# A gated recurrence on one core: the input's products cut into four column tiles, and TensorE's loop cut from sixteen steps to four

## The reference

```python
def step(h, x_t):
    fused = sigmoid(concat([x_t, h]) @ w_W + w_b)
    hidden_state, output_state = split(fused, 2)
    memory_state = x_t @ wx_W + wx_b + hidden_state * (h @ wh_W + wh_b)
    h_new = output_state * h + (1.0 - output_state) * tanh(memory_state)
    return (h_new, h_new)
return x + scan(step, cond_1024, x over time)
```

## Time and profile before

| | us |
|---|---|
| median of 3 runs | 1894.34 (1892.4 to 1894.72) |
| the profiled execution, its own time | 1895.98 |
| its span in the trace | 1893.4 |
| busy in the span: PE / PEld / DVE / ACT / POOL | 1859.9 / 1465.7 / 1169.8 / 821.2 / 371.0 |

### The profile page before, as it was taken

The page is one execution under the profiler, slowest core; times in us unless marked ns, Lnnn a source line. Parts: engine busy times, 40 slices in busy tenths (PEclk is TensorE's granted clock), DMA queues, the critical chain, the costliest instruction groups (busy, mean ns, idle before and its releaser), DMA issues.

```text
span 1893.4 us, 124703 instructions
## 1 busy us (share of the span) xinstructions
PE 1859.9 (98%) x52320; PEld 1465.7 (77%) x52320; DVE 1169.8 (62%) x6153; ACT 821.2 (43%) x3983; POOL 371.0 (20%) x1540
## 2 busy tenths in 40 slices
PE   8999999999999999999999999999999999999998
PEld 6777777777777777777777777777777777777776
DVE  3666666666666666666666666666666666666665
ACT  3444444444444444444444444444444444444444
POOL 0111111111111111111111111111111111111111
PEclk9999999999999999999999999999999999999999
DMA  4000000000000000000000000000000000000000
GB/s 152 15 4 15 15 15 15 9 9 15 15 15 15 4 15 15 15 15 4 15 15 15 15 9 9 15 15 15 15 4 15 15 15 15 4 15 15 9 9 9
DMA packets 36083, 29.94 MB, mean 16 GB/s; under 512 B 1616, under 2 KB 34384, under 8 KB 35664
## 3 DMA queue, kind: packets, MB, share of 16 engines
q1 hardware_dynamic: 35664, 23.10, 3.9%
HBM read 14.70 MB, written 8.39 MB: 12 GB/s over the span
## 4 chain that ended last, share of the span: by engine, by line
PE 96%; DVE 2%; DMA 1%; ACT 1%; SPq 0%; issue 0%; POOL 0%; POOLq 0%
PE ps L192 73%; PE ps L181 23%; DVE turned L284 1%; DMA x_sb<-in_x 1%; DVE h L307 0%; ACT h_by L241 0%; DVE pre_z L292 0%; DVE pre_r L288 0%; ACT h L246 0%; SPq L146 0%; SPq L152 0%; SPq L143 0%; SPq L150 0%; SPq L148 0%; SPq L149 0%
## 5 line engine op out<-in xcount | busy, mean ns | idle before, releaser
L192 PE MATMUL ps<-wh,h 128*8 128x128 f32 (+2 forms) x49152 | 1443.2, 273 | 22.5 <-DVE h L307 19.2
L192 PEld LDWEIGHTS ps<-wh,h 128*8 128x8 f32 x49152 | 1073.4, 90 | 260.1 <-DVE h L307 44.0
L284 DVE STREAM_TRANSPOSE turned<-ps 128x128 f32<-128x128 f32 (+1 forms) x2048 | 575.1, 281 | 510.6 <-PE ps L192 483.6
L237 ACT ACTIVATE m_by<-pre_r 128x16 f32<-128x16 f32 x1024 | 223.4, 218 | 894.5 <-DVE pre_r L288 894.5
L181 PEld LDWEIGHTS ps<-x_sb,wx 128*128 128x128 f32 x3168 | 392.3, 192 | 161.8 <-issue 161.8
L181 PE MATMUL ps<-x_sb,wx 128*128 (+1 forms) x3168 | 483.9, 292 | 5.6 <-DMA wx<-in_w_x 5.6
L362 POOL TENSOR_TENSOR add<-turned,bias_h 128x16 f32<-128x16 f32 x1024 | 237.4, 232 | 881.4 <-DVE turned L284 881.4
L307 DVE TENSOR_TENSOR_SCAN h<-h_by,h 128x48 f32<-128x48 f32 x1024 | 263.5, 257 | 152.9 <-ACT h L246 152.6
L241 ACT ACTIVATE h_by<-pre_z 128x16 f32<-128x16 f32 x1024 | 230.2, 225 | 160.0 <-DVE pre_z L292 131.2
L375 POOL TENSOR_TENSOR y<-x_sb,h 128x32 f32<-128x32 f32 x512 | 133.4, 261 | 637.5 <-DVE h L307 637.5
L246 ACT ACTIVATE h<-m_pre 128x32 f32<-128x32 f32 x1024 | 237.6, 232 | 0.0
(11 more groups left out here) (6 smaller groups left out, 0.6 us busy)
## 6 DMA issues: line engine op xcount, KB each, us to landing
x_sb<-in_x SPq DMA_DIRECT2D x32, 256.0 KB, 4.6
out_h<-y SPq DMA_DIRECT2D x32, 256.0 KB, 2.7
wx<-in_w_x SPq DMA_DIRECT2D x6, 512.0 KB, 5.8
wh<-in_w_h SPq DMA_DIRECT2D x4, 768.0 KB, 11.3
bias_x<-in_b_x SPq DMA_DIRECT2D x1, 6.0 KB, 3.2
bias_h<-in_b_h SPq DMA_DIRECT2D x1, 2.0 KB, 3.1
h<-in_h SPq DMA_DIRECT2D x1, 16.0 KB, 3.6
```

The lines of the kernel that those rows point to most:

```text
L192: mm = pe.matmul(ps[Q * j:Q * j + B, bank, 0:cols], h_of(s - 1 if s else S, k), wh[:, k, j, at:at + cols], start=(k == 0), stop=(k == KC - 1),
L237: act.activation(m_by[:, o, :, 1], pre_r[:, o, :], ACT.Sigmoid).then_inc(r_ready[o], 1)
L284: return dve.transpose(turned[:, o, g0:g1].rearrange("p g c q -> p (g c) q"), ps[:, bank, at:at + cols].rearrange("p (c q) -> p c q", q=Q))
```

## The change

What changes, engine by engine:

- **TensorE, x's products.** Each product is cut into four, 32 outputs each, one per column tile. A product `32x128` then has a stationary operand of 128 by 32 and 128 moving columns. Every step has exactly 3 of the old products, so 12 of the new, and the last step of a block has them too. They use three PSUM banks in turn, not two.
- **TensorE, the loop** has a body of four steps. So that its addresses are fixed, each of the four steps r reads x's weights from its own place `wx_step[:, r]` and its own copy of the next block's x, `x_next[:, r]`.
- **SP's queue** loads `wx_step` for every step (three chunks, 192 KB) four steps ahead, once the step that used the place has ended it (`x_used`, or `x_product` for the fourth), and the four copies `x_next` once a block. The x of two blocks ahead is loaded as before.
- **h** is a ring of four places, and VectorE waits every four steps for POOL's `y_added` of the step just before. Until now it waited every eight, for a step eight further back. `y` has two buffers, and POOL waits at each block's start for `x_loaded`, which TensorE did before.

```diff
+    RING = 4
-    X_FROM = [-(-len(x_list) * s // (STEPS - 1)) for s in range(STEPS)] + [len(x_list)]
-    X_PLAN = [x_list[X_FROM[s]:X_FROM[s + 1]] for s in range(STEPS)]
+    X_EACH = len(x_list) // STEPS
+    X_UNITS = RING * X_EACH // KC
...
+        x_next = sb("x_next", [P, RING, KC, TOK])
+        wx_step = sb("wx_step", [P, RING, X_EACH, P])
-        h = sb("h", [P, STEPS, HALVES, HALF])
-        y = sb("y", [P, KC, STEPS, B])
+        h = sb("h", [P, RING, HALVES, HALF])
+        y = sb("y", [P, 2, KC, STEPS, B])
...
+            for r in range(RING):
+                load_wx(r)
+                sp.dma_start(x_next[:, r], x_flat[:, :, TOK:2 * TOK]).then_inc(x_next_loaded[r], 16)
             sp.dma_start(x_sb[:, :, TOK:2 * TOK], x_flat[:, :, TOK:2 * TOK]).then_inc(x_loaded, 16)
...
+            def x_product_of(u, k, w, moving):
+                for j in range(TILES):
+                    at = slice(Q * j, Q * (j + 1))
+                    mm = pe.matmul(ps[at, X_BANK + u % X_UNITS, 0:TOK], w[:, at], moving,
+                                   start=(k == 0), stop=(k == KC - 1), tile_position=(0, Q * j))
+                if k == KC - 1:
+                    mm.then_inc(x_product, 1)
+                return mm
...
+            def x_products(i, s):
+                pe.wait_ge(wx_step_loaded[s], held(pe, i * 16 + 16))
+                pe.wait_ge(x_next_loaded[s], held(pe, (i // (STEPS // RING)) * 16 + 16))
+                for n in range(X_EACH):
+                    u, k = divmod(s * X_EACH + n, KC)
+                    if k == 0:
+                        pe.wait_ge(xg_ready, held(pe, i * X_UNITS + (UNITS - X_UNITS + u + 1)))
+                    last = x_product_of(u, k, wx_step[:, s, n, :], x_next[:, s, k, :])
...
-            with nc.Fori(0, BLOCKS, engines=(mybir.EngineType.PE,), hint_back_edge=True) as i:
...
-                pe.wait_ge(x_loaded, pe.snap(i * 16 + 16))
-                for s in range(STEPS):
+            with nc.Fori(0, T // RING, engines=(mybir.EngineType.PE,), hint_back_edge=True) as i:
+                t0 = pe.snap(i * RING)
+                for s in range(RING):
                     step(t0, s)
-                    x_products(X_PLAN[s], nxt_block, unit0)
+                    x_products(i, s)
...
-                if s % Y_HALF == 0:
-                    dve.wait_ge(y_added, held(dve, t0 + (s + Y_HALF)))
+                if s % RING == 0:
+                    dve.wait_ge(y_added, held(dve, t0 + (s + STEPS)))
```

More of the change, by code:

```diff
@@ L103, in build @@
         x_loaded = sem("x_loaded")
+        x_next_loaded = [sem(f"x_next_loaded{r}") for r in range(RING)]
+        wx_step_loaded = [sem(f"wx_step_loaded{r}") for r in range(RING)]
         y_stored = sem("y_stored")
@@ L117, in build @@
         x_product = sem("x_product")
+        x_used = [sem(f"x_used{r}") for r in range(RING - 1)]
         r_summed = halves("r_summed")
@@ L152, in _, with load_wx @@
                 sp.dma_start(wh[:, k], w_h[:, k]).then_inc(wh_loaded, 16)
-            sp.dma_start(x_sb[:, :, TOK:2 * TOK], x_flat[:, :, TOK:2 * TOK]).then_inc(x_loaded, 16)
-            def store(i):
+            def load_wx(s):
+                sp.dma_start(wx_step[:, s % RING], wx_flat[:, s * X_EACH:(s + 1) * X_EACH])\
+                    .then_inc(wx_step_loaded[s % RING], 16)
+            for r in range(RING):
+                load_wx(r)
+                sp.dma_start(x_next[:, r], x_flat[:, :, TOK:2 * TOK]).then_inc(x_next_loaded[r], 16)
+            sp.dma_start(x_sb[:, :, TOK:2 * TOK], x_flat[:, :, TOK:2 * TOK]).then_inc(x_loaded, 16)
+            with sp.Fori(0, BLOCKS) as i:
+                after = sp.snap((i + 2) % BLOCKS)
+                cols = bass.ds(sp.snap(after * TOK), TOK)
+                sp.wait_ge(x_loaded, sp.snap(i * 16 + 16))
+                sp.dma_start(x_sb[:, :, cols], x_flat[:, :, cols]).then_inc(x_loaded, 16)
+                for s in range(STEPS):
+                    if s % RING == 0:
+                        turn = sp.snap(i * (STEPS // RING) + (s // RING + 1))
+                    if s % RING < RING - 1:
+                        sp.wait_ge(x_used[s % RING], turn)
+                    else:
+                        sp.wait_ge(x_product, sp.snap(i * UNITS + (s // RING + 1) * X_UNITS + UNITS))
+                    load_wx((s + RING) % STEPS)
+                    if s >= STEPS - RING:
+                        sp.dma_start(x_next[:, s % RING], x_flat[:, :, cols]).then_inc(x_next_loaded[s % RING], 16)
                 sp.wait_ge(y_added, sp.snap(i * STEPS + 2 * STEPS))
@@ L167, in _ @@
[L167 to L170, removed]
+                             y[:, bass.ds(sp.snap(i % 2), 1)].rearrange("p a c t b -> p (a c) (t b)"))\
+                    .then_inc(y_stored, 16)
+            sp.wait_ge(x_loaded, (BLOCKS + 1) * 16)
+            for r in range(RING):
+                sp.wait_ge(wx_step_loaded[r], (T // RING + 1) * 16)
+                sp.wait_ge(x_next_loaded[r], (BLOCKS + 1) * 16)
@@ L172, in _ @@
+            sp.wait_ge(y_stored, 16 * (BLOCKS + 2))
         @block.tensor
         def _(pe):
[L174 to L179, removed]
-                        pe.wait_ge(wx_loaded[u * WX_PARTS // UNITS], 16)
[L181 to L184, removed]
+            def x_product_of(u, k, w, moving):
[6 more added lines that the diff above has]
+                return mm
@@ L364, in hidden, with add_x @@
                     .then_inc(hm_ready[o], 1)
-            def add_x(s, t0, nxt, after):
+            def add_x(s, t0, which, after):
                 if s == 0:
@@ L382, in step @@
                     hidden(o, s % 2, nxt)
-                add_x(s, t0, nxt, held(pool, t0 + (s + 2)))
+                add_x(s, t0, which, held(pool, t0 + (s + 2)))
             pool.sem_inc(y_added, STEPS)
```

49 lines of the change are left out of this document (25 added, 24 removed).

## The result

The changed kernel takes 1825.47 us (median of 4 runs, 1824.59 to 1825.9), the kernel before 1893.87 in the same series. The ratio is 0.9639, with a 95% interval of 0.9622 to 0.9656. The forecast was 1827.

The account below looks back on a forecast made before the run. TensorE was taken to bound steps with products of x, the recurrence, only 0.18 us shorter, the step without. From the 1894.3 us median: minus 87 for blocks, plus 19 for jumps, plus 1 for start and end, gives 1827 us (range 1812 to 1845).

Parts of the forecast that it names:

- Bound: TensorE bounds steps with products of x (3.61 us for three); the recurrence bounds the step without, its own period 3.47 us.
- x in column tiles: x slot: six quads take 0.66 us, 32-column loads hide, and up to about 0.3 us of tiling switches a step goes.
- The sum for a block: Block of 16 steps: 58.23 us becomes 55.52, so 2.71 less, and 87 less over 32 blocks.
- The jumps, +19 us: TensorE's four-step loop: the queue gets through the jump late, costing 0.15 us at each of 127 jumps.
- VectorE's wait, costed at nothing: VectorE's first transpose waits for POOL's addition every fourth step; 0.24 us of slack, so no cost.
- Loads and start: Weight loads on SP's queue stay hidden; x for POOL lands at 27 us; start and end add 1 us together.
- The hidden jump: Rival, chance 0.27: at TensorE's loop all goes as forecast but without the 19 us for jumps, giving 1808 us.
- the slot's 0.21 us is no matter of tiling: Rival, chance 0.07: it belongs to each stream's first weights; x slot stays 0.87 us, giving 1917, or 1879 with jumps hidden.
- The fetch of instructions (0.08): Rival, chance 0.08: each TensorE loop jump waits for one or two instruction packets of 1.1 us, giving 1950 to 2090 us.

Follow-up runs that it names:

- the run with five: Changed kernel with two more of x's products in each step, in column tiles, into a bank nobody reads: 1934.74 us, ratio 1.0213.
- the 14-page body: Changed kernel with a 16-step TensorE body, x's weights resident, and six of x's twelve products in four steps: 1825.91 us, ratio 0.9645.

## Why the prediction was right

**Bound.** Right. The step without products of x told what the recurrence allows, 3.47 us; measured are 3.48, with TensorE idle before its h passes. Two products in the slot changed nothing, and from the run with five follows the engine's own period with three, 3.27 us.

**x in column tiles.** Right, and close. The way between the two tilings was priced at up to about 0.3 us a step. The engine's own period with three products is 3.61 on the whole array and 3.27 in tiles, so it is 0.34. The quad of 0.11 us came as the rows of h had it, and the 32-column loads hide: four loads of 110 ns and four matmuls share each 0.11 us. The rule of the Trainium skill (TensorE: Matmul & The Clock Gate, Part 3, The mechanism) that loads overlap only where the row groups differ does not hold here, since all these loads use all 128 rows.

**The sum for a block** was -87 us for a step of 3.47. With 3.477, the mean distance of VectorE's first transposes in the undisturbed steps, it is -83.

**The jumps, +19 us.** This step failed: the h pass behind a jump was to start 0.19 us late, and it starts on time (3.48 us after the one before). The jumps cost 0. Two numbers in it were off, how far the queue runs ahead and what the branch takes. Here are the jump's instructions on TensorE's queue (ns min/median/max, start us), for the earlier trace rows:

```profile
L252 PEldq ALU_OP  x1: 32/32/32, 1005.3 to 1005.3; - x1
L252 PEldq COMPARE_BRANCH  x1: 216/216/216, 1005.4 to 1005.4; - x1
L252 PEldq BRANCH_PREFETCH_HINT  x1: 31/31/31, 1005.7 to 1005.7; - x1
L252 PEldq FUSED_REGOPS  x1: 50/50/50, 1005.8 to 1005.8; - x1
```

The queue comes to the jump at 1005.3, when the last of x's quads is still 0.5 us from its start (1005.27 plus 0.55). I had taken 0.33, from 16 records. 20 would have been right. And it is through at 1005.85, since the branch takes 216 ns. The h pass wants it at 1006.08. 375 ns was the price in a body whose pages are fetched anew, not of a branch as such. The prediction took it for free of any fetch. The kernel before fetched 13 pages in each turn, its branches took 375 ns in the median, those of the 14-page body 448, and those of the two bodies that stay in the store 216.

**VectorE's wait, costed at nothing.** This failed too: 0.07 us in steps 4, 8 and 12, 96 times, 7 us. The price stood in the trace of before. There the wait had its second place in step 8, and this row of VectorE's timeline is that step:

```profile
1046.31 0.32 DVE L284 STREAM_TRANSPOSE turned<-ps 128x128 f32<-128x128 f32 x1 [0.95 <-PE ps L192]
```

It has 0.95 us of idle time where the other steps' transpose has 0.88. It cost nothing then, because the slot of x hid it: the distance of the first transposes is 3.68 us up to that step and 3.54 behind it, around the 3.61 of the others. I had asked whether POOL was in time, and not what the wait itself costs.

**Step 2** of each block loses 0.06 to 0.07 us in VectorE's scan of half 0, 2 us in all. It does so in every run that the recurrence bounds, those with a body of 16 included; only where every step has the second wait does it add nothing. The cause stays open.

**Loads and start.** The loads are hidden with the short body: no wait in the changed kernel's trace ends on `wx_step` or `x_next`. The first x for POOL came at 29 us and not 27, and start and end cost 3 us, not 1: the second step began 1.9 us later than in the kernel before (32.42 and 30.52, by VectorE's first transpose), and from the last step's first transpose to the end it took 7.6 us and not 6.4.

So in spans: -83 for the step, +7 and +2 for VectorE, +3 for start and end make -71, and the spans differ by 70.6. The forecast of -67 came from -87 + 19 + 1. That the median is right within 2 us is luck: 19 us for jumps that cost nothing stood against four small terms, 15 us together, that I had at nothing or too low. The range and the sign rest on the part that held.

**Rivals.** The hidden jump is what came true, at 1825 and not at 1808. That the slot's 0.21 us is no matter of tiling fell with the run on the whole array, where it came back. The fetch of instructions (0.08) was no danger to the four-step body, since it stays in the store. But with a body of 16 steps it would have made the change slower than before, as two runs showed. Its price was not a packet for each jump, but a rate for all pages.

## What to carry to other kernels

A step of the kernel that happens to lack the work you want to shrink tells how much the shrinking can bring: read it first. When a wait or an instruction becomes part of the path, look for the same form elsewhere in the old trace, where it is hidden, and take its price from there. Count a loop body's instructions before you multiply them, since here column tiles made four of each product of x, and look at the instruction queue's packets per turn of the loop.

## What the runs showed of the hardware

- A body on TensorE of 1920 matmul and load instructions (8 steps) stayed in the store: 9 packets in the whole run, and a branch of 216 ns. One of 3264 (the kernel before) or more was fetched again in every turn, 13 to 16 packets of 16 KB. Bodies between these were not tried. The page Runtime: NRT & Kernel Launch of the Trainium skill (Instruction fetch mechanics) gives TensorE room for 2048 instructions, which agrees.
- Where pages were short, one came in 3.7 to 3.9 us. There the shortage showed at the jump, as a branch of 2.6 to 3.1 us in the median, and in some bodies as gaps of 0.2 to 0.3 us in the steps behind it. 14 pages in 56.0 us were just enough.
- A second wait in front of a transpose on which VectorE waits anyway became an instruction of its own and cost 0.07 us, though it was satisfied: 23 us with one in every step, and 7 us less when it stood on an instruction with no other wait.
- Matmuls with weights of 32 columns in four column tiles follow each other at 0.11 us a quad for 128 moving columns, with all 128 rows in use, and their loads of 110 ns hide.
- From h's column tiles to the whole array, the first weight load stood for about 0.33 us, once per slot (161.8 us in 481 times). The way there and back cost 0.34 us a step.
